# Two of four key-value products moved from TensorE to lane shuffles and multiply-adds on VectorE

## The reference

```python
qkv = einsum('oc,bchw->bohw', w_qkv, x)                       # 768 channels
agg = grouped_1x1(depthwise_5x5(qkv, w_dw), w_pw)             # 96 groups of 8
qkv_ms = concatenate([qkv, agg], axis=1)                      # 64 heads of 8 + 8 + 8
q, k = relu(...), relu(...)                                   # v as it is
v1 = concatenate([v, ones])                                   # 9 rows
vk = einsum('bhdn,bhen->bhde', v1, k)                         # 9 x 8 a head, over all points
out = einsum('bhde,bhen->bhdn', vk, q)
out = out[:, :, :-1] / (out[:, :, -1:] + EPS_ATT)
out = einsum('oc,bchw->bohw', w_proj, out)                    # then batch norm over all images, + residual
```

## Time and profile before

| | us |
|---|---|
| runs | 2483.9 median (2482.04 to 2485.74, 3 runs) |
| profiled execution | 2481.6, of it span 2479.8 |
| TensorE busy | 2262.2 (91%) |
| ScalarE busy | 914.8 (37%) |
| VectorE busy | 856.3 (35%) |
| GpSimd busy | 214.4 (9%) |
| mean granted TensorE clock | 0.96 of full |

### The profile page before, as it was taken

How to read it: one execution, slowest core, us unless ns; L and a number is a source line. 1 busy time by engine, 2 the same in 40 slices (tenths; PEclk the granted TensorE clock), 3 DMA queues, 4 the chain that set the end, 5 groups by cost and what they waited for, 6 DMA issues and landing times. The chain is left out here.

```text
span 2479.8 us, 33369 instructions
## 1 busy us (share of the span) xinstructions
PE 2262.2 (91%) x13760; PEld 1632.0 (66%) x13760; DVE 856.3 (35%) x1340; ACT 914.8 (37%) x1957; POOL 214.4 (9%) x207
## 2 busy tenths in 40 slices
PE   7999999998799999999999999999999999999720
PEld 6888888887566666666666666666666666676410
DVE  4667676667111231141132114113211411411352
ACT  4443443443333423423433342343334234333142
POOL 2223312221000000000000000000000000000000
PEclk9999999999899999999999999999999999999865
DMA  2110111100657655654664675466476547545678
GB/s 100 77 77 15 62 77 77 77 39 39 252 192 259 218 190 195 228 198 162 225 213 169 222 243 189 156 224 225 152 245 217 201 154 237 197 153 208 244 289 358
DMA packets 130790, 437.23 MB, mean 176 GB/s; under 512 B 6224, under 2 KB 105168, under 8 KB 112464
## 3 DMA queue, kind: packets, MB, share of 16 engines
q1 hardware_dynamic: 129488, 416.22, 47.3%
q0 software_dynamic: 1152, 18.87, 1.8%
HBM read 260.29 MB, written 174.78 MB: 175 GB/s over the span
## 5 line engine op out<-in xcount | busy, mean ns | idle before, releaser
L715 PE MATMUL cv<-work,wc 128*64 128x288 f32 x4608 | 620.2, 412 | 0.0
L715 PEld LDWEIGHTS cv<-work,wc 128*64 128x64 f32 x4608 | 303.7, 136 | 234.0 <-issue 31.6
L1077 DVE TENSOR_TENSOR wc<-pwe,dwe 128x512 f32<-128x512 f32 x288 | 181.2, 687 | 788.1 <-PE cv L715 772.5
L696 PE MATMUL pj<-x,wqkv 128*128 128x288 f32 x1536 | 388.6, 410 | 22.2 <-DMA x<-scratch_x 22.2
L696 PEld LDWEIGHTS pj<-x,wqkv 128*128 128x128 f32 x1536 | 289.6, 191 | 110.4 <-issue 35.5
L928 ACT ACTIVATE work<-cv 128x288 f32<-128x288 f32 x384 | 158.5, 413 | 515.2 <-PE cv L715 515.2
L909 ACT COPY work<-pj 128x288 f32<-128x288 f32 x384 | 154.1, 401 | 289.9 <-PE pj L696 289.3
L732 PE MATMUL vk<-kvT 128*128 128x129 f32 x1248 | 202.1, 285 | 8.1 <-ACT kvT L945 4.9
L753 PE MATMUL tr<-ident,work 128*128 128x128 f32 x1248 | 196.9, 282 | 10.4 <-issue 8.9
L753 PEld LDWEIGHTS tr<-ident,work 128*128 128x128 f32 x1248 | 138.5, 142 | 89.7 <-issue 85.9
L732 PEld LDWEIGHTS vk<-kvT 128*128 128x128 f32 x1248 | 163.8, 191 | 23.7 <-ACT kvT L945 9.8
(11 more groups left out here) (104 smaller groups left out, 2877.3 us busy)
## 6 DMA issues: line engine op xcount, KB each, us to landing
work<-scratch_padded SPq DMA_DIRECT2D x48, 2599.5 KB, 10.6
scratch_padded<-work SPq DMA_DIRECT2D x48, 1300.0 KB, 6.0
scratch_phases<-work SPq DMA_DIRECT2D x96, 576.0 KB, 3.4
work<-scratch_phases SPq DMA_DIRECT2D x64, 576.0 KB, 4.7
x<-scratch_x SPq DMA_DIRECT2D x9, 2304.0 KB, 10.5
scratch_x<-xs SPq DMA_DIRECT2D x8, 2304.0 KB, 6.9
q<-scratch_phases SPq DMA_DIRECT2D x32, 576.0 KB, 4.6
xs<-in_x SPq DMA_DIRECT2D x7, 2304.0 KB, 8.9
```

The source lines that it names most:

```text
L696: mm = nc.tensor.matmul(pj[:, c % 2, :PLANE], wqkv[:, kc, u, :], x1[:, kc, c * PLANE:(c + 1) * PLANE], start=(kc == 0), stop=(kc == CT - 1))
L715: mm = nc.tensor.matmul(cv[64 * b:64 * b + 64, j % 2, :PLANE], wc[:, 2 * j + b, dy].rearrange("p c o -> p (c o)"), window, start=(dy == 0) ...
L1077: op = nc.vector.tensor_tensor(wc[:, blocks, dy], pwe[:, u, blocks].rearrange("p g (c o) -> p g c o", o=1).to_broadcast([P, HB, DIM, NG]), ...
```

## The change

Products 1 and 3, those of convolved keys and values, leave TensorE, except product 3 of the last image. In their place `spin` on VectorE takes them in 16 steps: a step shuffles the lanes of the values within each group of 16, for one half of the points, and multiplies them with the keys and sums the result. After 8 shifts of both halves every value row has met every key row of its head. A `tensor_reduce` gives the sums of the keys. The steps are cut into shares that stand between VectorE's other work. GpSimd builds its masked matrix from the 9 numbers a lane (`vkd`).

Since `kva` is then read for longer, units 2 and 3 are stored to memory at once, but loaded later, behind unit 5's `replicate`; `phases` and its semaphores are there twice. The weights that `wc` is made of are no longer held for all units, but loaded unit by unit into `taps`, two units ahead. `vkraw` moves into the common work space. The turns and projections of the small matrices stand at other places.

```diff
-SEG = (0, DG, DG + AG, 2 * DG + AG)
-NTR = 2 * (DG + AG)
+SEG = (0, None, DG, 2 * DG)
+NTR = 2 * DG
+SPIN = HW // 2
+SPINS = [[lane // 16 * 16 + 2 * k + lane % 2 for lane in range(32)] for k in range(DIM)]
...
-        pwe = sb("pwe", [P, NU, NB, DIM])
-        dwe = sb("dwe", [P, NU, NB, KROWS, NG])
+        taps = sb("taps", [P, 2, NB, DIM + KROWS * NG])
...
+        spun = sb("spun", [P, 2, SPIN])
+        sums = sb("sums", [P, 2, DIM])
+        vkd = sb("vkd", [P, 2, DIM + 1])
...
             def image(i, nxt):
                 for u in range(NU):
-                    lay_out(i, u)
+                    if u + 2 < NU or nxt:
+                        ahead, v = unit_at(i, u + 2)
+                        sp.wait_ge(wc_ready, 2 * (i * NU + u) + 2)
+                        sp.dma_start(taps[:, v % 2], dram["taps"][v]).then_inc(taps_in[v % 2], 16)
+                    lay_store(i, u)
+                    if u not in (2, 3):
+                        lay_load(i, u)
                     if u == 3 and nxt:
                         sp.wait_ge(pj_filled, i * (NU * NG) + NU * NG)
                         sp.dma_start(x1[:], dram["x1"][i + 1]).then_inc(x_in, 16)
                     if u + 2 < NU or nxt:
                         replicate(*unit_at(i, u + 2))
+                    if u == 3:
+                        lay_load(i, 2)
+                        lay_load(i, 3)
...
                         if u == 0 and prev:
+                            if j == 4:
+                                turn_product(i - 1, 3)
+                            if j == 5:
+                                project_product(i - 1, 3)
                             product(i, 0, shares(DG, 0, 8)[j])
...
                         if u == 2:
-                            product(i, 1, shares(AG, 0, 4)[j])
-                            product(i, 2, shares(DG, 4, 8)[j])
-                        if u == 4:
-                            if j == 0:
-                                project_product(i, 1)
+                            product(i, 2, shares(DG, 0, 8)[j])
+                        if u == 5 and i == last_image:
                             product(i, 3, shares(AG, 0, 8)[j])
-                        if u == 5 and j == 3:
-                            turn_product(i, 3)
+                        if u == 4 and j == 0:
+                            turn_product(i, 1)
+                        if u == 4 and j == 2:
+                            project_product(i, 1)
+                        if u == 4 and j == 4:
+                            turn_product(i, 2)
+                        if u == 4 and j == 6:
+                            project_product(i, 2)
...
+            def spin(i, p, share):
+                first = (2 * i + p // 2) * 16
+                kc, vc = kva[:, 0], kva[:, 1]
+                if share[0] == 0:
+                    for u in (PRODUCTS[p][0], PRODUCTS[p][0] + 1):
+                        for h in range(2):
+                            dve.wait_ge(lay_done[u % 2][h], laid_at(i, u))
+                def turn(t):
+                    piece = slice(t // DIM * SPIN, (t // DIM + 1) * SPIN)
+                    wait_count(dve, spun_summed, first + t - 1)
+                    nc.vector.stream_shuffle(spun[:, t % 2], vc[:, piece], SPINS[t % DIM]).then_inc(spun_ready, 1)
+                def add(t):
+                    piece = slice(t // DIM * SPIN, (t // DIM + 1) * SPIN)
+                    out = (sums[:, 0] if t < DIM else sums[:, 1])[:, t % DIM:t % DIM + 1]
+                    dve.wait_ge(spun_ready, first + t + 1)
+                    nc.vector.scalar_tensor_tensor(out=spun[:, t % 2], in0=kc[:, piece], scalar=1.0, in1=spun[:, t % 2],
+                                                   op0=ALU.mult, op1=ALU.mult, accum_out=out).then_inc(spun_summed, 1)
+                for t in share:
+                    if t == 0:
+                        turn(0)
+                    if t + 1 < 16:
+                        turn(t + 1)
+                    add(t)
+                if share[-1] == 15:
+                    wait_count(dve, dsel_ready, 4 * (i - 1) + p + 1)
+                    nc.vector.tensor_reduce(vkd[:, p // 2, DIM:DIM + 1], kc, AX.X, ALU.add)
+                    dve.wait_ge(spun_summed, first + 16)
+                    nc.vector.tensor_tensor(vkd[:, p // 2, 0:DIM], sums[:, 0], sums[:, 1], ALU.add).then_inc(vkd_ready, 1)
...
-                for u in range(2, NU):
-                    weights(i, u)
-                    if prev and u - 1 in Y_CHUNKS:
-                        statistics(i - 1, Y_CHUNKS[u - 1])
+                weights(i, 2)
+                if prev:
+                    statistics(i - 1, Y_CHUNKS[1])
+                spin(i, 1, range(0, 6))
+                weights(i, 3)
+                spin(i, 1, range(6, 10))
+                if prev:
+                    statistics(i - 1, Y_CHUNKS[2])
+                spin(i, 1, range(10, 16))
+                weights(i, 4)
+                if i != last_image:
+                    spin(i, 3, range(0, 5))
+                if prev:
+                    statistics(i - 1, Y_CHUNKS[3])
+                weights(i, 5)
+                if i != last_image:
+                    spin(i, 3, range(5, 13))
+                    weights(i + 1, 0)
+                    spin(i, 3, range(13, 16))
```

More of the change, by code:

```diff
@@ L529, in phase_l1 @@
         spread = sb("spread", [P, 2, 4, P], F32R)
-        qpad, rep, kva, stage = cut(work, (2, QPAD), (2, NB * PADDED + ROW), (2, HW), (2, HB // 2, PLANE))
+        qpad, rep, kva, stage, vkraw = cut(work, (2, QPAD), (2, NB * PADDED + ROW), (2, HW), (2, HB // 2, PLANE), (2, P + 1))
         rcp = work[:, 5 * CT * HW:5 * CT * HW + 2 * CHUNK]
         kvT = sb("kvT", [P, 2, 2, 2, P + 1])
-        vkraw = sb("vkraw", [P, 2, P + 1])
         vkm = sb("vkm", [P, 2, P])
@@ L611, in _ @@
         def _(sp):
-            for dst, name in ((wqkv, "wqkv"), (pwe, "pwe"), (dwe, "dwe")):
-                sp.dma_start(dst[:], dram[name]).then_inc(w_first, 16)
+            sp.dma_start(wqkv[:], dram["wqkv"]).then_inc(w_first, 16)
+            for u in range(2):
+                sp.dma_start(taps[:, u], dram["taps"][u]).then_inc(taps_in[u], 16)
             sp.dma_start(x1[:], dram["x1"][0]).then_inc(x_in, 16)
@@ L674, in _ @@
             sp.wait_ge(cv_filled, NIMG * NU * NG)
-            for h in range(2):
-                sp.wait_ge(lay_done[h], laid_at(NIMG - 1, NU - 1))
-            sp.wait_ge(tr_filled, NIMG * NTR)
+            for u in (NU - 2, NU - 1):
+                for h in range(2):
+                    sp.wait_ge(lay_done[u % 2][h], laid_at(NIMG - 1, u))
+            sp.wait_ge(tr_filled, NIMG * NTR + AG)
+            sp.wait_ge(vkd_ready, 2 * NIMG - 1)
+            sp.wait_ge(dsel_ready, 4 * NIMG)
             sp.wait_ge(q_copied, 2 * NIMG)
@@ L720, in product @@
             def product(i, p, groups):
-                u, source, half = PRODUCTS[p]
-                last = (DG if source == 0 else AG) - 1
+                u, source, _ = PRODUCTS[p]
                 base = i * NTR + SEG[p]
+                last = groups_of(p) - 1
                 def step(g):
@@ L781, in denominators @@
                     pe.wait_ge(cv_freed, (i + 1) * NU * NG)
-                    for h in range(2):
-                        pe.wait_ge(lay_done[h], laid_at(i, NU - 1))
+                    for u in (NU - 2, NU - 1):
+                        for h in range(2):
+                            pe.wait_ge(lay_done[u % 2][h], laid_at(i, u))
                     pe.wait_ge(q_copied, 2 * (i + 1))
@@ L931, in product @@
             def product(i, p, groups):
-                _, source, _ = PRODUCTS[p]
-                last = (DG if source == 0 else AG) - 1
                 base = i * NTR + SEG[p]
@@ L1036, in _, with masked @@
             pool.wait_ge(w_in, 16 * NW)
[L1038 to L1050 removed]
+            def masked(i, p):
+                source = PRODUCTS[p][1]
+                spread_in = source == 1 and not (i == last_image and p == 3)
+                if not spread_in:
+                    pool.wait_ge(vk_freed, 2 * i + (p + 1) // 2 + 1)
+                    whole, total = vkraw[:, raw_slot(p), 0:P], vkraw[:, raw_slot(p), P:P + 1]
+                else:
+                    pool.wait_ge(vkd_ready, 2 * i + p // 2 + 1)
+                    whole = vkd[:, p // 2, 0:DIM].rearrange("p (x c h) -> p x c h", x=1, h=1).to_broadcast([P, NG, DIM, 2])
+                    total = vkd[:, p // 2, DIM:DIM + 1]
+                shape = (lambda a: a.rearrange("p (x c h) -> p x c h", x=NG, c=DIM)) if spread_in else (lambda a: a)
+                wait_count(pool, sa_filled, 4 * i + p - 1)
+                nc.gpsimd.tensor_tensor(shape(vkm[:, p % 2, :]), shape(mask8[:, source]), whole, ALU.mult).then_inc(vkm_ready, 1)
+                wait_count(pool, den_filled, NDEN * i)
+                nc.gpsimd.tensor_tensor(dsel[:, slot_of(p)].rearrange("p e h -> p (e h)"),
```

(19 more changed lines are left out.)

147 lines of the change are left out of this document (67 added, 80 removed).

## The result

The changed kernel takes 2499.14 us (median of 4 runs, 2497.61 to 2502.59), the kernel before 2482.97 beside it on the same chip (4 runs, 2481.54 to 2485.74): 1.0058 of the time, 95% interval 1.0044 to 1.0073. It is slower, as forecast, but by 0.6% where 2.0% was forecast (2534). The profiled execution has a span of 2495.8, 16.0 more than before.

What follows compares the result with a forecast made beforehand. TensorE was taken to bound the kernel. The profiled 2481.6 us + 55.8 (six images) + 8 (first) - 10.5 (last) - 3.2 (start) = 2531.7, with 2.3 to the runs' median 2534; range 2452 to 2580.

Steps and rivals of the forecast that it cites:

- the landing of the `kva` loads: Loads behind the `rep` load on SP's queue land at T4 + 22.5, bounds T4 + 20 and T4 + 25.
- The first share: VectorE's work from the `kva` landing through product 3's first steps to half of unit 5's weights: 19.5 us.
- unit 5 to unit 0: VectorE's remaining weights, eight steps and next weights behind unit 5's convolution: 26.6 us, where TensorE needs 19.7.
- My upper bound: A VectorE step takes at most 3.1 us, if the multiply-add's extra over the usual rate grows with size.
- my line: VectorE's usual rate from earlier rows: 1.034 ns an element, so 1152 elements cost 1.36 us.
- +8: First image: its shorter unit 3 lengthens the waits by some 10 us, less `kva` waits leaving TensorE's queue.
- The start: Only 512 KB instead of 1536 KB of convolution weights ahead of TensorE's first x load: -3.2 us.
- The last image: Product 3 stays on TensorE beside unit 5's convolution, with no projections behind: -10.5 us.
- The 1.7 of the sum: Clock cost per image, in us, of TensorE's lower granted clock after a wait.
- Rival 1: Shuffle or multiply-add on VectorE takes two cycles an element: step 4.05 us, kernel about 2675; chance 0.13.
- Rival 2: `kva` loads do not lie behind the `rep` load, land about T4 + 11: kernel about 2454; chance 0.10.
- Rival 3: VectorE never holds TensorE up: kernel some 2330 us; chance 0.04.

Runs made afterwards that it cites:

- e5: The e1 kernel with unit 4's query loads also moved behind the next image's unit 0 `rep` load: 2343.39 us, 0.9427 of the kernel before.
- e1: The changed kernel with the four `kva` loads issued ahead of the x load on SP's queue: 2380.96 us, 0.9584 of the kernel before.
- e3: The changed kernel with the `kva` loads issued between unit 5's padded store and the `rep` load: 2435.44 us, 0.9805 of the kernel before.
- e2: The changed kernel with unit 5's weights ahead of product 3's first share on VectorE: 2478.39 us, 0.9970 of the kernel before.
- e4: The changed kernel without the 16 shuffles and 16 multiply-adds of products 1 and 3: 2363.21 us, 0.9514 of the kernel before.
- e6: The kernel before with only the taps loaded unit by unit: 2486.35 us against 2486.66, ratio 1.0000.
- e7: The changed kernel with only product 1 on VectorE, product 3 on TensorE in every image, `kva` loads still late: 2401.13 us, 0.9656 of the kernel before.

## Why the prediction was right, and where it was off

**The mechanism held, step by step.** TensorE's own work was to fall to 193.4 an image; without waits it is 193.97 (e5), mostly for unit 4, 22.3 for my 21.6. VectorE was to idle 27 us in front of product 3's first shuffle (26.9), held by a load of `kva`; TensorE's busy share was to fall to 87% (86%) and VectorE to be busy some 147 us (140.5); two waits were to stand before units 5 and 0, and none at T4. All of that is in the trace after from the second image on; the first image has a wait at T4 (below). e1 and e3 show the cause by moving the landing alone, e2 that unit 5's weights need not stand behind the steps for the stall to come, e4 that it is the steps behind the late landing that cost, and e1 and e5, with all steps in place, that their number is not.

**The step that failed is a term of the sum, the landing of the `kva` loads: set at T4 + 22.5, measured at T4 + 19.7.** What the change does to an image is a small difference of two large numbers (19 us of work gone, 20 and 7 us of waits put in its place), so an error of a tenth in the waits is nearly a third of the 9.3 us forecast. I took the rate from the `rep` load and the y store of before, 306 KB/us. The windows of the 16 DMA engines, where both were full, show that this pair was a poor sample; first the kernel before with `rep` load and y store, then the changed one with `rep` load and `kva` loads, and a y store behind them (the last two columns: DMA share, GB/s):

```profile
1211.42:1220.42 9.00, 9.00 (x71) 5.67 (x68) 1.89 (x3) 3.41 (x7) 0.00 (x0) 1.00 0.96 333
```

```profile
1208.37:1214.37 6.00, 6.00 (x48) 3.15 (x45) 0.00 (x0) 1.52 (x5) 0.00 (x0) 1.00 0.95 403
1214.37:1220.37 6.00, 6.00 (x31) 3.97 (x31) 0.00 (x0) 2.26 (x6) 0.00 (x0) 1.00 0.99 349
```

At about the same share the engines moved 333 GB/s there and 403 and 349 here; why the rates differ no run shows. The 4904 KB landed 16.4 us after the `rep` load's issue, which with my 3 us for start and landing (no run measures these by themselves; the smallest transfer of before, 2 KB of `gb`, landed 1.8 us after its issue) is 366 KB/us: T4 + 19.7, just outside the bound of T4 + 20. This is 2.8 of the 5.4 us by which the image was overestimated (this one: 216.85 for 222.3).

**The other terms.** The first share was priced 19.5 and took 18.7 (1221.76 to 1240.42), unit 5 to unit 0 26.6 and took 25.4, both mostly because a step is 2.73 and not 2.85: I had charged ScalarE's 187 ns for reading a sum out, and on VectorE it is 83. My upper bound had a slip: the multiply-add of 256 elements lies 45 ns over my line, not 60, so the bound was 3.05 and not 3.1; nothing else hangs on it. T0 to T4 with the clock came to 153.1 for 153.7. So -2.8 - 0.8 - 1.2 - 0.6 makes the 5.4. In the mean image it is 4.7, and 28 us over six, of the 34 by which the profiled execution stayed under the forecast (2497.6 for 2531.7).

In the first image I had +8 and it was -1.3. The 4.8 us of landing and steps are in it too. Its wait goes in two parts, where I had set one of 30:

```profile
765.45 3.15 PE L746 MATMUL cv<-work,wc 128*64 128x288 f32 x12 [7.05 <-issue]
...
805.42 3.15 PE L746 MATMUL cv<-work,wc 128*64 128x288 f32 x12 [15.64 <-issue]
```

The first part is a wait at T4, which I had excluded. Unit 3 lasts 20.2 us in the first image before, and I had the weights of unit 4 ready at T3 + 22.5, behind product 1's last steps; that they would be late there follows from my own numbers. They came at T3 + 27.2, and without the steps (e4) this wait is not there. I haven't taken the remaining 4.5 us of the first image apart further.

The start was to give 3.2. TensorE's wait for x fell by 2.3. But the first phase, which the change doesn't touch, happened to end 4.4 later in this execution (TensorE comes to that wait at 613.0 before, 617.4 after, 613.2 in e6, 619.7 in e5), and from the first projection to the first convolution it took 1.0 less; so the sum shows +1.1. The last image gave 11.5 for my 10.5.

**The clock.** The 1.7 of the sum is 4 us at 0.42 below the full clock, from the 0.58 of the earlier trace rows. After the wait before unit 5 and after the one before unit 0 the first windows of 4 us show a granted clock of 0.50:

```profile
1240.42:1244.42 4.00, 4.00 (x18) 2.27 (x20) 4.00 (x6) 0.41 (x1) 0.00 (x0) 0.50 0.93 277
1244.42:1248.42 4.00, 4.00 (x36) 2.55 (x34) 3.91 (x8) 0.82 (x2) 0.00 (x0) 1.00 0.93 316
...
1265.79:1269.79 4.00, 4.00 (x16) 2.07 (x16) 4.00 (x6) 0.41 (x1) 0.00 (x0) 0.50 0.93 233
```

The first costs nothing, since the stretch to unit 0 is set by VectorE: its six instructions for unit 0's weights start at 1263.80 and take 3.69 us, and TensorE starts at 1265.79, when three are done. Behind the second unit 0 takes 42.2 to 43.7 instead of 40.9 (three images of e5 and all but the first of e7, without a wait): 1.3 to 2.8 for my 1.7. Not every such wait has this price. In e4 the waits before unit 0 are 0.5 to 3.2 us; behind five of the seven, one of 2.9 among them, the granted clock stayed at 1.00 and unit 0 took 40.9 to 41.0, behind the other two (2.7 and 3.2) it was 0.57 and 0.65 over the first 4 us and unit 0 took 42.5.

**The rivals.** Rival 1, an operation at half rate, fell at once: 1342 ns for 1152 elements is 1.16 ns an element with everything included, and twice the 1.034 ns an element of my line would be 2.4 us. Its 0.13 was my estimate; no row of before has this form, two fp32 sources in SBUF and a sum output. The shuffle took 1443 ns, 0.08 us over the 1.36 of my line. This hardly shows in the step, since the multiply-add starts 1.34 behind the shuffle. Rival 2's place in the queue is not what the change does, but e3 tried its landing and gave about its time (2435 for 2454, with the terms above as much too large). Rival 3, no hold-up at all, 2330, is what e5 reaches with two edits on SP's queue: 2343.

## What to carry to other kernels

Work that moves off the bounding engine is worth what it took only if whatever the new engine does behind it is not late; so look first at what stands ahead of the work's own inputs in the DMA queue, and only then at whether the engine has room. Here 141 us of work fitted into 194 without a wait, and four loads of 576 KB that stood behind the x load, the padded store with SP's wait for it, and the `rep` load of 2600 KB turned a gain of 4.2% (e1) into a loss of 0.6%. And when a stall ends in one place, look at the next releaser: after the first reordering it was the padded store, whose repair gave another 1.6%.

## What the hardware showed that I had not expected

- A multiply-add with two fp32 operands in SBUF and a sum output took 1342 ns for 128x1152, where the line of the earlier trace rows gives 1.36 us; reading its sum out took 83 ns on VectorE, where ScalarE's takes 187.
- A lane shuffle of 128x1152 fp32 took 1443 ns, and loading its mask 14 ns.
- The DMA engines, at 95% to 99% busy, moved from 333 to 403 GB/s with different transfers under way.
- Two loads of 576 KB ahead of a store of 1300 KB delayed it twice: in its issue, by 3.1 us, and again in its landing, 10.2 us instead of 7.1 (e1 and e5).
